# Four-layer network on one core: in the second layer the zero fill and the rank matmuls go first, and VectorE's scan pieces are placed anew

## What is computed

```python
ek = exp(min(k, 30)); ekv = ek * v
a = a * decay + ekv_t        # forwards and backwards: nf, nb
b = b * decay + ek_t         # forwards and backwards: df, db
euk = exp(min(u + k, 30))
num = nf + nb - ekv + euk * v
den = df + db - ek + euk
base = sigmoid(r) * (num / max(den, 1e-8))
```

```python
logits = x @ router_w
expert_idx = argmax(logits); score = sigmoid(max(logits))
xs = x * score
for e in range(8):
    m = expert_idx == e
    h = silu(xs[m] @ gate_w[e]) * (xs[m] @ up_w[e])
    out[m] += h @ down_w[e]
shared = silu(x @ shared_gate_w) * (x @ shared_up_w) @ shared_down_w
```

## Time and profile before

| | us |
|---|---|
| median of 3 runs | 1021.62 (1020.59 to 1023.24) |
| the profiled execution's own time | 1019.41 |
| its span in the profile | 1017.7 |
| mean granted TensorE clock | 0.897 of full speed |

### The profile page before, as it was taken

One profiled execution on the slowest core, in us unless ns is written; L12 is line 12 of the kernel. 1 busy time (PEld: TensorE's weight loads), 2 busy tenths in 40 slices (PEclk: granted clock), 3 DMA queues, 4 the chain that ended last, 5 costly groups with the idle time before them and its releaser, 6 DMA issues. The chain is left out here.

```text
span 1017.7 us, 11188 instructions
## 1 busy us (share of the span) xinstructions
PE 786.0 (77%) x3629; PEld 588.3 (58%) x3629; DVE 592.2 (58%) x1268; ACT 384.1 (38%) x832; POOL 236.5 (23%) x216
## 2 busy tenths in 40 slices
PE   0776557656556625659999999999986999999995
PEld 0332435523233411448888788888876788888884
DVE  6889699369878377644655655555553333333333
ACT  2300512212122258645454454454453333343332
POOL 0401000140100347022012012012001255554543
PEclk9887778578988759869999999999996899999998
DMA  4000000731111500030010010100002231314321
GB/s 132 0 2 0 1 0 1 298 120 31 32 31 37 187 4 1 1 124 9 34 43 5 38 42 1 43 0 2 1 1 63 75 104 52 104 52 104 94 48 41
DMA packets 37374, 49.85 MB, mean 49 GB/s; under 512 B 18670, under 2 KB 30038, under 8 KB 35654
## 3 DMA queue, kind: packets, MB, share of 16 engines
q1 hardware_dynamic: 36262, 46.90, 14.8%
q0 software_dynamic: 768, 2.10, 0.6%
q10 hardware_dynamic: 288, 0.14, 0.1%
HBM read 43.00 MB, written 6.13 MB: 48 GB/s over the span
## 5 line engine op out<-in xcount | busy, mean ns | idle before, releaser
L2029 DVE TENSOR_TENSOR B_l<-bank,TW_l 128x512 f32<-128x512 f32 (+1 forms) x50 | 34.6, 692 | 140.8 <-PE bank L1974 140.8
L1648 ACT ACTIVATE EX<-EX,nm 128x128 f32<-128x128 f32 (+1 forms) x128 | 57.2, 448 | 108.5 <-DVE nm L1697 107.9
L1598 POOL TENSOR_TENSOR WL<-RAW,WH 128x512 fp32r<-128x512 f32 x32 | 41.1, 1290 | 231.6 <-ACT WH L1622 231.6
L2064 POOL TENSOR_TENSOR HL_l<-H_l,HH_l 128x512 fp32r<-128x512 f32 (+1 forms) x50 | 64.1, 1283 | 119.9 <-ACT HH_l L2043 119.9
L1974 PE MATMUL bank<-XH,WH_l 128*128 128x512 f32 (+1 forms) x200 | 79.8, 399 | 0.0
L1974 PE MATMUL bank<-XL,WH_l 128*128 128x512 f32 (+1 forms) x200 | 79.5, 398 | 0.0
L1974 PE MATMUL bank<-XH,WL_l 128*128 128x512 f32 (+1 forms) x200 | 79.5, 398 | 0.0
L134 POOL TENSOR_TENSOR WV<-EUK,V 128x512 f32<-128x512 f32 x16 | 23.5, 1475 | 178.4 <-DVE GAIN L219 178.4
L1711 DVE TENSOR_TENSOR AL<-bank,AH 128x256 fp32r<-128x256 f32 x64 | 27.1, 424 | 62.1 <-ACT AH L1663 62.1
L1751 PE MATMUL bank<-XH,WH 128*128 128x512 f32 x128 | 59.5, 465 | 3.9 <-DVE XL L1454 3.9
L2051 ACT ACTIVATE S_l<-bank 128x512 f32<-128x512 f32 (+1 forms) x50 | 30.1, 601 | 83.9 <-PE bank L1974 83.9
(11 more groups left out here) (307 smaller groups left out, 2089.9 us busy)
## 6 DMA issues: line engine op xcount, KB each, us to landing
RAW<-l_attn SPq DMA_DIRECT2D x8, 1024.0 KB, 5.0
WE<-l_experts SPq DMA_DIRECT2D x1, 6144.0 KB, 19.8
RAW_l<-l_experts SPq DMA_DIRECT2D x9, 512.0 KB, 3.9
TW_l<-routed SPq DMA_DIRECT2D x16, 256.0 KB, 5.2
RAW<-l_w SPq DMA_DIRECT2D x3, 1024.0 KB, 7.2
TW_l<-routed SPq DMA_DIRECT2D x14, 192.0 KB, 3.2
RAW_l<-l_experts SPq DMA_DIRECT2D x9, 256.0 KB, 4.7
sorted_x<-ZERO SPq DMA_DIRECT2D x1, 1920.0 KB, 24.4
```

The source lines that it names most:

```text
L1598: pool.tensor_tensor(WL[:, slot, c], RAW[:, slot, c], WH[:, slot, c].bitcast(F32), ALU.subtract).then_inc(w_low, 1)
L1648: act.activation(EX[:, s, a:b], EX[:, s, a:b], ACT.Exp, bias=nm[:, s, i:i + 1], scale=scale, accum_out=rs[:, s, i:i + 1]).then_inc(expd, 1)
L2029: v.tensor_tensor(self.B[0:rows, q % 2], self.k.banks[2 * (q % 2) + 1][0:rows], self.TW[0:rows, w % self.TWS, n * W:(n + 1) * W], ALU.mult ...
L2064: pool.tensor_tensor(self.HL[0:rows, q % 4], self.H[0:rows, q % 2], self.HH[0:rows, q % 4].bitcast(F32), ALU.subtract).then_inc(self.h_low, 1)
```

## The change

In the second layer SP issues the zero fill before WS and WE. PE does the rank matmuls before `shared_up(0)`. The 32 pieces are dealt out anew: 2 (chunk 8 `den`, `num`) behind `cond_vector`; 1 (chunk 8 `add`) between HOT and the wait for the rank matmuls; 1 (chunk 8 `divide`) and then 4 (chunk 9), one behind each product of the shared expert; 17 over the 15 tiles (chunks 10 to 13 and `den` of chunk 14); 3 behind the last tile (the rest of chunk 14). The last 4, chunk 15, go into the third layer: `den` behind the instruction at L1300, `num`, `add` and `divide` behind the clips of t = 0, 1 and 2 (the last behind `out(0)`). POOL's product for chunk 15 moves to the third layer, behind L1178. PE's wait at L1098 falls away.

```diff
--- before.py
+++ after.py
@@ -726,14 +726,30 @@
             yield c, what
 
 
-PIECES1 = list(gain_pieces())
-STEPS1 = 4
+PIECES = list(gain_pieces())
+
+
+LOGITS1, RANKS1, START1, MIDDLE1, END1 = 2, 1, 5, 17, 3
+FIRST_PIECE2 = LOGITS1 + RANKS1 + START1 + MIDDLE1 + END1
 
 
 def pieces_after(j):
 
-    left = len(PIECES1) - STEPS1
-    return PIECES1[STEPS1 + left * j // TILES1:STEPS1 + left * (j + 1) // TILES1]
+    at = LOGITS1 + RANKS1 + START1
+    return PIECES[at + MIDDLE1 * j // TILES1:at + MIDDLE1 * (j + 1) // TILES1]
+
+
+def gain_pieces_done(v, k, pieces):
+    for c, what in pieces:
+        g = GainVector(v, k, c)
+        if what == "den":
+            g.den_scans()
+        elif what == "num":
+            g.num_scans()
+        elif what == "add":
+            g.add()
+        else:
+            g.divide()
 
 
 def layer1(nc, k, io):
@@ -811,13 +827,13 @@
         @block.sync
         def _(sp):
             sp.dma_start(RW[:], io["l1_router"]).then_inc(r_in, 16)
+
+            sp.wait_ge(made, 1)
+            sp.dma_start(xs_d.rearrange("(j p) d -> p j d", p=P),
+                         ZERO[:].rearrange("p (o d) -> p o d", o=1).to_broadcast([P, TILES1, D])).then_inc(zeroed, 16)
             sp.dma_start(WS[:], io["l1_experts"][0]).then_inc(ws_in, 16)
             sp.dma_start(WE[:].rearrange("p (e c) -> p e c", e=E1),
                          io["l1_experts"][1:].rearrange("e p c -> p e c")).then_inc(we_in, 16)
-
-            sp.wait_ge(made, 1)
-            sp.dma_start(xs_d.rearrange("(j p) d -> p j d", p=P),
-                         ZERO[:].rearrange("p (o d) -> p o d", o=1).to_broadcast([P, TILES1, D])).then_inc(zeroed, 16)
 
             def load(j):
                 if j >= RING1:
@@ -859,7 +875,7 @@
                 pool.wait_ge(xtok, t + 1)
                 pool.indirect_dma_start(xs_d, bass.IndirectOffsetOnAxis(ap=SLOT[:, t:t + 1], axis=0), XTOK[:, t],
                                         None).then_inc(scat, 16)
-            for c in range(FIRST_GAIN1 + 2, LAYERS * NCH):
+            for c in range(FIRST_GAIN1 + 2, LAYERS * NCH - 1):
                 gain_pool(pool, k, c)
             for n in range(RING1):
 
@@ -925,6 +941,9 @@
         def _(v):
             cond_vector(v, k, cond, 1, acc)
 
+            at = LOGITS1
+            gain_pieces_done(v, k, PIECES[:at])
+
             v.wait_ge(logits, 1)
             v.tensor_reduce(top[:], lg, AX.X, ALU.max).then_inc(rt, 1)
             v.wait_ge(rt, 1)
@@ -936,6 +955,9 @@
             v.tensor_reduce(kmax[:], KEY[:], AX.X, ALU.max).then_inc(rt, 1)
             v.wait_ge(rt, 4)
             v.tensor_tensor(HOT[:], KEY[:], each(kmax[:]), ALU.is_equal).then_inc(rt, 1)
+
+            gain_pieces_done(v, k, PIECES[at:at + RANKS1])
+            at += RANKS1
 
 
             v.wait_ge(hot_sum, 1)
@@ -960,30 +982,21 @@
             v.tensor_copy(SLOT[:], place[:]).then_inc(pos, 1)
             v.tensor_scalar(EID[:], which[:], float(E1 - 1), float(WCOLS1), ALU.min, ALU.mult).then_inc(pos, 1)
 
...
-            for q in range(STEPS1):
+            gain_pieces_done(v, k, PIECES[at:at + START1 - 4])
+            at += START1 - 4
+            for q in range(4):
 
                 v.wait_ge(s_silu, q + 1)
                 v.tensor_tensor(HS[:, q], SS[:, q % 2], shared_banks[q % 2][1][:], ALU.mult).then_inc(s_h, 1)
-                piece(*PIECES1[q])
+                gain_pieces_done(v, k, PIECES[at + q:at + q + 1])
             for j in range(TILES1):
 
                 v.wait_ge(silu, j + 1)
                 if j >= 2:
                     v.wait_ge(h_turned, j - 1)
                 v.tensor_tensor(HT[:, j % 2], ST[:, j % 2], banks[j % 2][:, F1:2 * F1], ALU.mult).then_inc(h, 1)
-                for c, what in pieces_after(j):
-                    piece(c, what)
+                gain_pieces_done(v, k, pieces_after(j))
+            gain_pieces_done(v, k, PIECES[FIRST_PIECE2 - END1:FIRST_PIECE2])
 
         @block.tensor
         def _(pe):
@@ -1009,9 +1022,6 @@
                                        start=(i == 0), stop=(i == KD - 1))
                 mm.then_inc(s_up, 1)
 
-            pe.wait_ge(ws_in, 16)
-            shared_up(0)
-
             pe.wait_ge(rt, 5)
             pe.wait_ge(consts, E1 + 3)
             pe.matmul(rank[:], BEFORE[:], HOT[:], start=True, stop=False, skip_group_check=True)
@@ -1022,6 +1032,8 @@
                 mm = pe.matmul(total, ALL[:], HOT[:, t], start=(t == 0), stop=(t == NT - 1), skip_group_check=True)
             mm.then_inc(hot_sum, 1)
 
+            pe.wait_ge(ws_in, 16)
+            shared_up(0)
             pe.wait_ge(xtok, 4)
             shared_up(1)
             for q in (2, 3):
@@ -1094,8 +1106,6 @@
                     if m == 0:
 
                         pe.wait_ge(y, TILES1 - (TILES1 - 1 - n) % 2)
-                    else:
-                        pe.wait_ge(k.g_done, LAYERS * NCH)
                     for f in range(2):
                         w = WS[:, DOWN1 + f * D + m * P:DOWN1 + f * D + (m + 1) * P]
                         pe.matmul(acc[2 * m + n][:], w, HS[:, 2 * f + n], start=(f == 0), stop=False,
@@ -1176,6 +1186,7 @@
             pool.tensor_scalar(RAW[:, 2], RAW[:, 2], SW[:, 2:3], ROUND, ALU.mult, ALU.add).then_inc(dround, 1)
             pool.wait_ge(dround, 1)
             pool.tensor_scalar(RAW[:, 2], RAW[:, 2], ROUND - 1.0, ROUND + 1.0, ALU.max, ALU.min).then_inc(dclip, 1)
+            gain_pool(pool, k, LAYERS * NCH - 1)
 
             pool.wait_ge(ln_in, 16)
             for t in range(NT):
@@ -1298,6 +1309,8 @@
             maxima(NT - 1)
 
             v.tensor_scalar(ms[:], ss[:], 1.0 / FF2, 1e-6, ALU.mult, ALU.add).then_inc(post, 1)
+            rest = PIECES[FIRST_PIECE2:]
+            gain_pieces_done(v, k, rest[:1])
             v.wait_ge(root, 1)
             v.reciprocal(rstd[:], rt[:]).then_inc(post, 1)
             v.wait_ge(post, 2)
@@ -1325,6 +1338,7 @@
                 v.tensor_scalar(H[:, t], H[:, t], ROUND - 128.0, ROUND + 127.0, ALU.max, ALU.min).then_inc(hc, 1)
                 if t >= 2:
                     out(t - 2)
+                gain_pieces_done(v, k, rest[1 + t:2 + t])
             out(NT - 2)
             out(NT - 1)
 
```

More of the change, by code:

```diff
@@ L961, in _ @@
             v.tensor_scalar(EID[:], which[:], float(E1 - 1), float(WCOLS1), ALU.min, ALU.mult).then_inc(pos, 1)
[L963 to L970, removed]
-                else:
-                    g.divide()
-            for q in range(STEPS1):
+            gain_pieces_done(v, k, PIECES[at:at + START1 - 4])
+            at += START1 - 4
+            for q in range(4):
                 v.wait_ge(s_silu, q + 1)
                 v.tensor_tensor(HS[:, q], SS[:, q % 2], shared_banks[q % 2][1][:], ALU.mult).then_inc(s_h, 1)
-                piece(*PIECES1[q])
+                gain_pieces_done(v, k, PIECES[at + q:at + q + 1])
             for j in range(TILES1):
```

## The result

The changed kernel's median is 1024.57 us (1020.29 to 1028.53, 20 runs) beside 1019.88 (1014.94 to 1026.02, 20 runs) for the kernel before on the same chips: a ratio of 1.0043, with a 95% interval from 1.0027 to 1.0059. A later comparison on another chip gave 1.0058 (1.0037 to 1.0079). So the change makes the kernel about half a per cent slower.

The account below looks back on a forecast made before the run. PE's work plus the XIN load round trip was taken to bound the tiles, DVE's queue the third layer's tail. Terms -7.6 - 1.5 + 1.3 + 9.4 = +1.6 us on 1021.6 gave 1023.2; range 1018.2 to 1026.6.

Parts of the forecast that it names:

- the start: Second layer up to the first tile's transposition: earlier fill, rank matmuls and scatters gain 7.6 us, bounds 6.4 and 9.
- the tail: Third layer behind the mean square: chunk 15's pieces delay H, covered only by 2.23 us of waiting; +9.4 us, bounds 7 and 11.9.
- The slots and the first scatter: Second layer's start: slots ready at 202.2, first scatter 6.4 us earlier, 2.9 from the fill and 3.5 from the rank matmuls.
- The eight scatters end before chunk 9's additions: gain 1.7.: Second layer's start: scatters end at 213.0, so additions no longer hold one; gain 1.7 us, less 0.4 for scans.
- The tiles: Second layer's 15 tiles: fewer pieces gain nothing as DVE was no bound; the last tile's prompt HT gives -3.7 us.
- Behind the tiles: Second layer's gathers: additions hold the fourth by 1.8 us, scans cost 0.4; -1.5 in sum with the last HT's gain.
- rival had 0.15: Second layer's scatters and gathers: additions hold none, the fourth scatter was long for another reason; -0.2 us, 1021.4, chance 0.15.
- Third layer's product: Third layer behind L1178: POOL's product for chunk 15 slips in ahead of L1280 and holds it; +1.3 us, bounds 0 and 1.3.
- rival 1: Third layer's tail: clock stays low for the products of t = 2, 4 and 6; total +4.0 us, 1025.6, chance 0.22.
- Rival 3: Second layer's tiles: fewer of the 15 run at the low clock; -3.4 us in total, 1018.2, chance 0.15.
- Rival 4: Second layer's start: DVE's add or late HS hold slots or tile 0, gaining 3 less; +4.6 us, 1026.2, chance 0.08.
- the stated sign of being wrong: Block lengths: wrong if the third layer grows by less than 6 us or the second shrinks by more than 11.

Follow-up runs that it names:

- e2: The kernel before with the zero fill alone put first, pieces where they were; ratio to the kernel before 1.0000 (0.9980 to 1.0019).
- e3: The kernel before with the rank matmuls alone put first, pieces where they were; ratio to the kernel before 0.9993 (0.9966 to 1.0020).
- e8: Zero fill and rank matmuls first, no pieces beside scatters or behind the last two tiles, 28 behind 13 tiles, none in the third layer; 0.9924 to the kernel before.
- e5: The changed kernel with POOL's product for chunk 15 back in the second layer; ratio to the kernel before 1.0046 (1.0026 to 1.0066).
- e9: The changed kernel with chunk 15's den, num at the second layer's end, add, divide before the third layer's first product, POOL's product back; 1018.43 us, 0.9990 to the kernel before.
- e6: The changed kernel with chunk 15 back in the second layer, 24 pieces behind the first 13 tiles, none behind the last two; 1015.67 us, 0.9941 to the kernel before.
- e1: The changed kernel with chunk 15 and its POOL product back in the second layer, 21 pieces over the tiles; 1018.02 us, 0.9971 to the kernel before.
- e7: The kernel before with only chunk 15's four pieces and POOL product moved to the third layer; 1028.47 us, 1.0082 to the kernel before.
- e4: The kernel before with zero fill and rank matmuls both put first, pieces where they were; ratio to the kernel before 0.9930 (0.9903 to 0.9956).

## Why the prediction was right or wrong

The forecast was 1023.2, with a range from 1018.2 to 1026.6; 1024.6 lies in it. But the likeliest case was a change within 0.3% (0.55), and the interval of the ratio is mostly above that, where the prediction saw a chance of 0.26. The forecast of +1.6 us is too low by about 3: the two big terms, the start and the tail, are right in kind, the start is 2 to 3 us too large, and the total lies in the range by its width, which is partly luck. Step by step:

- **The slots and the first scatter.** 3.5 us for the rank matmuls and 2.9 for the fill: measured 3.52 at the slots, and neither alone is kept, as stated (e2, e3). The first scatter moved by 5.5, not 6.4: POOL begins 0.9 us after the slots are there, which I had reckoned as nothing.
- **"The eight scatters end before chunk 9's additions: gain 1.7."** This term failed. They began 0.9 later, three of the first seven took 0.3 to 0.45 more beside scans or the product of `divide`. So the eighth began inside the additions and was held in five of six profiles, while in the sixth an addition was. The hold was moved and not removed. First transposition: -5.7 in the first profile, -4.6 in the other five, for -7.6.
- **The tiles.** "DVE was no bound, so nothing" holds: ahead of the last tile the kernels with 17 and with 28 pieces differ by 0.6 us in the mean, and e8, with 28 in 13 tiles, took 99.3 us over all 15. The prompt last HT gave 3.9 us in both profiles of the changed kernel, for a forecast 3.7; but in e5 and e9, with the same order, only 2.5 and 2.2 of it are there, as the last tile ran partly at the low clock.
- **Behind the tiles.** Forecast 2.2 us lost, measured 1.6, but by other terms: the additions, which I had priced at 1.8, cost the third and fourth gathers 0.1; the scans cost the first two 0.7; and 0.8 is the first gather's later start, of which 0.5 and 0.7 are found in e6 and e8 too, with VectorE idle. The Trainium skill's rule in "SBUF — State Buffer", section "Who interferes with whom", was right for the gathers, whose rival had 0.15. It doesn't cover the scatters of e1. It says that two SBUF inputs contend with what GpSimd reads; that an indirect DMA reads its indices in SBUF is a possible way to fit both, and no run here tries it.
- **Third layer's product.** "The product holds L1280": shown (e5), at 0.9 us instead of 1.3.
- **Third layer's tail.** 9.4 forecast and 9.4 measured in both profiles of the changed kernel, 9.4 in e7. The cover was the 2.23 us of waiting, of which 0.19 were left, and nothing else in the round: H of t = 3 is 8.6 us late for a reckoned 8.7. Of the products of t = 2, 4 and 6 only the first ran at the low clock (1.85), the others at 1.05, so rival 1 did not come. e9 shows the reason for two of the four pieces: `add` and `divide` in a gap cost 0.3 us.
- **Not in the sum:** 1.7 us between executions in the third layer's first stretch, and 7 in the tiles, both by the clock. The one profile of the kernel before (a span of 1017.7) was not extreme in either, but the first of the changed kernel was favourable in the tiles. With the other profile of the changed kernel the stretches give 37.0 + 102.9 + 17.7 + 64.1 + 35.0 = 256.7 against 250.5, +6.2, which fits 1.0058.
- **Rival 3** (fewer tiles at the low clock) happened in the first profile and is no effect of the change. **Rival 4** had the right size by the wrong mechanism: the start gave less, but neither `add` nor HS was late.
- **The signs.** `out(0)` all but without a wait, no wait for HT at the last tile and a held L1280 (2.16 us for the stated 2.4 or more) came; a gather of over 2 us did not (the longest under additions took 1.05 in the changed kernel). The second layer shrank by 11.0 us in the first profile, which just escapes the stated sign of being wrong, and by the clock's luck: 5.9 in the second profile.

## What to carry to other kernels

Before work is moved into an engine's idle time, ask whether that idleness is a gap ahead of something that comes late anyhow (6.1 us before the first silu: 0.3 paid for 6.6 of work) or a turn of a round in which this engine hands on to the next (the tail: 9.4 us paid for 11.2 of work). Two waits that end within a few microseconds of one another can be worth little one by one and much together (1.4 and 1.3 us against 6.8 here): test both edits at once before either is thrown away. And when work is moved past a hold, look where it lands: here the held scatter was simply another one.

## What was not expected of the hardware

POOL's first indirect DMA starts 0.9 us after its last condition where that is the slots (slots at 203.80, scatter at 204.68), the same in e1 and e4; in the kernel before, where the landing of the zero fill came last, it was 0.3 (208.4 and 208.70). The third layer's first stretch falls into two groups, 61.5 and 63.1 us, in kernels that have the same code there, by whether the granted clock rises 2.6 to 4.1 or 7.5 to 9.3 us behind PE's first matmul of gate and up. And the tiles of one order of work take from 98.9 to 106.3 us, as single tiles run partly at the lower clock level: a single profile can mislead by more than the effect that is looked for.
